# Some 230 pieces of a fused two-layer kernel at other places in the orders of five engines

## The reference

```python
h = layernorm(x)*(1+ca)+sa;  x = x + ga * attention(h)     # layer 0: 4 heads, dilations 1, 2, 4, 8
h = layernorm(x)*(1+cb)+sb;  x = x + gb * ffn(h)           # input and weight rounded to a 6-bit grid
h = layernorm(x)*(1+ca)+sa;  x = x + ga * mamba(h)         # layer 1
h = layernorm(x)*(1+cb)+sb;  x = x + gb * gated_recurrence(h)
# mamba: projection, convolution over 4 tokens, silu, then per channel (512) and state (16)
#   state = exp(dt*A)*state + dt*B*xc ;  y = sum over states of C*state
#   y = (y + D*xc) * silu(z) ; output projection
# gated_recurrence: over the 4 sequences b as steps:
#   c = sigmoid(wf x + uf c + bf)*c + sigmoid(wi x + ui c + bi)*tanh(wc x + uc c + bc)
#   out[b] = tanh(wo x[b] + uo c_final + bo)
```

## Time and profile before

| | |
|---|---|
| median of 3 runs | 1270.32 us (1268.75 to 1272.96) |
| span of the profiled execution | 1264.5 us, 12574 instructions |
| time of that execution beside its span | not recorded; median less span is 5.8 us |
| PE, DVE, POOL, ACT busy | 1140.8, 1155.2, 982.6, 795.0 us |
| mean granted clock of PE | 0.986 of full speed |
| first scan starts | 97.6 us |

### The profile page before, as it was taken

One profiled execution on the slowest core, in us unless ns is written; L12 is line 12 of the kernel. 1 busy time (PEld: TensorE's weight loads), 2 busy tenths in 40 slices (PEclk: granted clock), 3 DMA queues, 4 the chain that ended last, 5 costly groups with the idle time before them and its releaser, 6 DMA issues.

```text
span 1264.5 us, 12574 instructions
## 1 busy us (share of the span) xinstructions
PE 1140.8 (90%) x3612; PEld 640.1 (51%) x3612; DVE 1155.2 (91%) x1138; ACT 795.0 (63%) x1445; POOL 982.6 (78%) x712
## 2 busy tenths in 40 slices
PE   7989678998999899997999899997999899789996
PEld 5636333664457444764457443763457443444453
DVE  3768999999999999899999999899999999999987
ACT  2256567765786668755786668755786667655532
POOL 3216886889778887989778997889778996976862
PEclk9999989999999999999999999999999999899998
DMA  7308588766868688866878679876868786899922
GB/s 285 115 16 315 176 269 284 278 233 233 281 226 297 200 278 292 289 233 225 290 219 301 197 277 311 276 241 217 292 217 287 215 282 236 290 335 346 374 86 116
DMA packets 92309, 313.87 MB, mean 248 GB/s; under 512 B 10432, under 2 KB 15680, under 8 KB 91984
## 3 DMA queue, kind: packets, MB, share of 16 engines
q1 hardware_dynamic: 89936, 306.26, 70.3%
q10 hardware_dynamic: 2304, 6.82, 1.5%
HBM read 301.73 MB, written 11.31 MB: 248 GB/s over the span
## 4 chain that ended last, share of the span: by engine, by line
PE 43%; DVE 22%; POOL 14%; ACT 9%; issue 8%; DMA 3%; SPq 0%; DVEq 0%; POOLq 0%; ACTq 0%
PE ps L907 13%; DVE ps L1741 12%; POOL arena L1970 8%; PE ps L601 5%; PE ps L830 4%; PE ps L609 3%; DVE arena L1749 3%; DMA arena<-bc_scratch 2%; PE ps L647 2%; PE ps L751 2%; PE ps L723 2%; ACT ps L1295 2%; ACT arena L931 2%; PE ps L728 1%; PE ps L633 1%
## 5 line engine op out<-in xcount | busy, mean ns | idle before, releaser
L1970 POOL TENSOR_TENSOR arena<-arena 128x1024 f32<-128x1024 f32 x255 | 600.3, 2362 | 136.5 <-PE ps L907 113.2
L1741 DVE TENSOR_TENSOR_SCAN ps<-ps,arena 128x1024 f32<-128x1024 f32 (+1 forms) x257 | 585.8, 2280 | 30.3 <-ACT ps L1295 17.9
L907 PE MATMUL ps<-arena,identF 128*128 128x512 f32 x1024 | 482.8, 603 | 49.0 <-DVE arena L1749 29.4
L1295 ACT ACTIVATE ps<-arena,negA 128x512 f32<-128x512 f32 x512 | 332.7, 683 | 83.2 <-DVE arena L1749 78.2
L907 PEld LDWEIGHTS ps<-arena,identF 128*128 128x128 f32 x1024 | 190.3, 193 | 267.2 <-issue 208.8
L1749 DVE TENSOR_TENSOR arena<-ps,arena 128x1024 f32<-128x1024 f32 (+1 forms) x257 | 312.0, 1214 | 5.9
L922 ACT ACTIVATE arena<-arena,rnln 128x256 f32<-128x256 f32 x118 | 61.9, 589 | 42.1 <-POOL rnln L1776 24.9
L647 PE MATMUL ps<-arena,inw 128*128 128x512 f32 x128 | 60.0, 614 | 11.7 <-ACT arena L931 9.6
L1307 ACT ACTIVATE arena<-ps 128x2 f32<-128x2 f32 x128 | 22.0, 172 | 64.9 <-DVE arena L1749 64.4
L931 ACT ACTIVATE arena<-ps,modT 128x512 f32<-128x512 f32 x43 | 51.7, 1266 | 14.7 <-PE ps L474 12.6
L728 PE MATMUL ps<-arena,inw 128*128 128x512 f32 x128 | 60.2, 592 | 0.0
(11 more groups left out here) (222 smaller groups left out, 1707.1 us busy)
## 6 DMA issues: line engine op xcount, KB each, us to landing
arena<-bc_scratch SPq DMA_DIRECT2D x511, 512.0 KB, 5.0
arena<-in_x SPq DMA_DIRECT2D x16, 256.0 KB, 6.9
arena<-in_x SPq DMA_DIRECT2D x8, 512.0 KB, 8.4
xr_scratch<-arena SPq DMA_DIRECT2D x6, 512.0 KB, 6.9
px_scratch<-arena SPq DMA_DIRECT2D x6, 512.0 KB, 6.1
out_x<-arena SPq DMA_DIRECT2D x5, 512.0 KB, 2.6
arena<-bc_scratch SPq DMA_DIRECT2D x9, 256.0 KB, 3.6
woT<-in_woT SPq DMA_DIRECT2D x4, 512.0 KB, 10.0
```

The source lines that it names most:

```text
L907: x = pe.matmul(ps[:, Y, :], identF[:], inp[:, m % RING, q, :], start=False, stop=(i == BLOCK_STEPS - 1 and q == 1), skip_group_check=True)
L1295: x = act.activation(ps[:, 2 * (m % 2) + q, :], dt[:, kd, :], ACT.Exp, scale=negA[:, kd, 2 * i + q:2 * i + q + 1])
L1741: x = dve.tensor_tensor_scan(states, states, inp[:, m % RING, q, :].rearrange("p q t -> p (q t)"), 0.0, ALU.mult, ALU.add)
L1970: x = pool.tensor_tensor(inp[:, m % RING, :, :], u[:, kd:kd + 1, :].broadcast_to([P, 2, TH]), b_at[:, m % 3, :, :], ALU.mult)
```

## The change

Only the table `TIMES` is changed. It issues the same instructions; the pieces of the chains stand at other places in each engine's order. The part of the diff that the text speaks of:

```diff
 TIMES = {
-    "sp_before": {"x_in": -7, "bc_out": 30.5, "dt_in": 30.5},
-    "sp_after": {"xr_out": 11.75, "px_out": 28.25},
+    "sp_before": {"x_in": -7.25, "bc_out": 30, "dt_in": 21.75},
+    "sp_after": {"xr_out": 16.25, "px_out": 35.75},
...
-    "pe_before": {"hn1_t0": -2.25, "hn1_t1": -2.25, "q0": -2, "k0": -2, "s0": 2, "q1": 2, "k1": 3.75, "v0": 5.25,
-        "s1": 6, "att0": 7, "v1": 7, "att1": 10.25, "op0": 11, "op1": 11, "xd_t0": 20, "xd_t1": 20,
-    "pe_second": {"hn1_t0": 2.25, "hn1_t1": 2.25, "q0": 3, "k0": 3, "s0": 3, "q1": 3, "k1": 7.25, "v0": 8.25,
+    "pe_before": {"hn1_t0": -2.5, "hn1_t1": -15, "q0": -1.75, "k0": -4.75, "s0": 2.75, "q1": -10.5, "k1": 4.25,
+        "v0": 5.25, "s1": 6, "att0": 8, "v1": -10.25, "att1": 11.25, "op0": 11.5, "op1": -14, "xd_t0": 20, "xd_t1": 11,
+    "pe_second": {"hn1_t0": 3.25, "hn1_t1": 5, "q0": 1, "k0": 5.25, "s0": 1, "q1": -20.5, "k1": -2.5, "v0": 3,
+        "s1": -14.25, "att0": 7.75, "v1": 8, "att1": 10.25, "op0": 11, "op1": -1.5, "xd_t0": 19.5, "xd_t1": 4.25,
...
-    "act_before": {"hn1": (-3.5, -3.5), "hB1": (-2.25, -2.25), "q0": 0, "k0": 0, "q1": 3.25, "exp0a": 4.25,
-        "exp0b": 4.25, "k1": 4.25, "v0": 7, "exp1a": 7, "exp1b": 7, "att0": 9, "v1": 9, "att1": 10.75,
-        "x_proj": 28.75, "first_decay": (35, 37.75), "softplus": (33.75, 34.25), "dt_copy": 37.75, "xc_silu": 28.5},
-    "act_second": {"hn1": (-10.5, -10.5), "hB1": (6, 6), "q0": 6.25, "k0": 6.25, "q1": 7, "exp0a": 7,
-        "softplus": (33.75, 33.75), "dt_copy": 41.25, "xc_silu": 28.5},
+    "act_before": {"hn1": (-3.5, -11), "hB1": (-2.25, -19), "q0": -0.75, "k0": -3.75, "q1": 3.75, "exp0a": 1,
+        "exp0b": 1.25, "k1": -0.75, "v0": 6.5, "exp1a": 4.5, "exp1b": -8.25, "att0": 9.25, "v1": -7.25, "att1": 11.5,
+        "hn3": (24, 18.5), "hB3": (24.75, 16.25), "xc_init": (25.75, 23.75, 27.75, 24.5), "x_proj": 29.25,
+        "first_decay": (35.75, 42.25), "softplus": (34, 20.25), "dt_copy": 40.25, "xc_silu": 22.5},
+    "act_second": {"hn1": (-8.5, -19.25), "hB1": (6.5, 0.75), "q0": -2.5, "k0": 2, "q1": 5.25, "exp0a": -17,
+        "first_decay": (34.75, 51.25), "softplus": (34.25, 32.5), "dt_copy": 28, "xc_silu": 24.75},
...
-    "dve_before": {"ln1_stats": -4.5, "ln1_moments": -4, "smax": (2.5, 6.5), "rsum": (6.5, 8.75), "ln2_stats": 13.25,
-        "ln3_moments": 22.5, "pad": 25.75, "conv": (26.75, 26.75, 26.75, 28, 28, 28)},
-    "dve_second": {"ln1_stats": -13.5, "ln1_moments": -11.25, "smax": (6.75, 9), "rsum": (9, 9.5),
-    "dve_after": {"ln4_stats": 6.25, "z": (6.5, 7.75, 8.25, 9.75), "ln4_moments": 6.5},
+    "dve_before": {"ln1_stats": -3.75, "ln1_moments": -16.75, "smax": (2.5, 5.75), "rsum": (7, 7.5), "ln2_stats": 13,
+        "ln3_moments": 22.75, "pad": 12.5, "conv": (26.75, 16, 9.75, 28.25, 25.5, 23.5)},
+    "dve_second": {"ln1_stats": -9.25, "ln1_moments": -16.75, "smax": (-6.75, -11.5), "rsum": (6.75, 8.75),
+    "dve_after": {"ln4_stats": 6.25, "z": (5.5, 8, 8.5, 9.25), "ln4_moments": 6},
...
-        "ffn_add": (20, 20), "ln3_rstd": 22, "u": (35, 37), "cut": (35, 37)},
-    "pool_after": {"cp_gate": -7.25, "cp_add": (5, 5), "ln4_rstd": 6.75, "f_c": 21, "i_g": 25.5, "c_new": 25.5},
+        "ffn_add": (19.75, 15.25), "ln3_rstd": 22, "u": (33.75, 40.75), "cut": (35.25, 44.5)},
+    "pool_after": {"cp_gate": -10.25, "cp_add": (4.75, -22.5), "ln4_rstd": 6.25, "f_c": 20.25, "i_g": 26,
+        "c_new": 17.5},
```

33 lines of the change are left out of this document (16 added, 17 removed), and 11 rows, old and new, of the table TIMES.

## The result

The changed kernel takes 1277.24 us (median of 6 runs, 1275.79 to 1283.82) against 1269.53 us for the one before on the same chip (6 runs, 1267.51 to 1272.96): a ratio of 1.0074, 95% interval 1.0047 to 1.0101. It is slower; I had said 1267.7. They are more than the 7.7 between the medians: the traced execution of the kernel before was one of its fastest. Of its 70 executions beside the experiments three had a span under 1265 us; the median span on each of the four chips was 1266.7 to 1267.5.

What follows compares the result with a forecast made beforehand. DVE was taken to set the pace, its idle time being what could be won. 5.6 - 7.0 - 1.2 = -2.6 on the span 1264.5, plus 5.8, gave 1267.7 us; 8-in-10 range 1259 to 1277.

Steps and rivals of the forecast that it cites:

- Term 1: Start, first overlapped attention (half 1): chained evictions delay scans 0 and 1; +5.6 us by scan 8, between +3 and +9.
- The rule that I set beside it: Start, PE: after idling it runs at half rate, so waits between chained projections could add up to 2.9 us.
- term 2: Five steady seams, halves 2 to 6: three edits bring scan 28 forward; -1.4 us a seam, -7.0 in all.
- no drain: Seam's Exp table load: a skill rule gives 1.28 plus a drain, 2.66 us; the rows showed only 1.28.
- the sign of term 2: What would show the seam gain: a steady half of 142 us instead of 143.3.
- the gain stands: Steady seam to scan 40: saturated PE passes its earlier q0 on, coming 1.6 us earlier at the second c_proj.
- rival 2: ACT's order between decays 31 and 38 takes the seam back, 0.4 us lost a seam; 1277 us, chance 23%.
- I cost them at nothing: Other moved pieces (SP's later stores, POOL's gating, cuts): readers come 10 us later, so 0 us.
- Term 3: Seam of half 1: exponentials and copy leave decays 30 and 37, easing scan 30's 2.00 us wait; -1.2 us.
- The 5.8 us: Difference between profiled span 1264.5 and median 1270.32, taken as time lying around a span and added to the forecast.
- My range: Whole kernel: 1259 to 1277 us, meant to hold the time 8 times in 10.
- the sign: Whole kernel: the outcome that the change makes it slower, chance 23%.

Runs made afterwards that it cites:

- experiment 1: Kernel before with the changed table for half 1 alone: 1283.48 us; with z's entries of the block beside it changed too: 1275.03 us, ratio 1.0055.
- experiment 7: Kernel before with silu ahead of decay 24 and the next half's statistics behind the convolution's second part: 1268.15 us, ratio 0.9985; each alone: 1267.17 and 1274.72 us.
- Experiment 6: Changed kernel with the copy of dt and two small exponentials back at their old ScalarE place in halves 3, 5 and 7: 1282.31 us, ratio 1.0094.
- experiment 5: Changed kernel with SyncE's store of xr back: 1275.71 us; with all SyncE pieces and GpSimd's three weight gating products back: 1276.68 us, ratio 1.0063.
- experiment 3: Kernel before with the changed tables for the last block's output pieces (steps 224 to 255) alone: 1271.20 us, ratio 1.0017.

## Why the prediction was wrong

**Which part was right.** Term 1: 5.9 us at scan 8 for 5.6, and experiment 1 shows that the debt stays. That nothing gives it back was wrong by 1.1 us at step 16: a wait of 0.76 in the trace before, just ahead of scan 12, took a part. The rule that I set beside it (half rate for the other projections too, up to 2.9 us) did not come to pass for q1 and k1: these took 2.9 and 3.0 us at a granted clock of 1.00 (2.4 GHz), where I had put 2.9. In term 2 the step at scan 28 was right (-1.7 said, -2.0 measured), with its three edits and its chain through the columns, q0, the read-out and i_g. So were the waits that I listed after it: 1.4 at scan 32 (1.22 in the even halves, 1.42 in the odd ones), none at the gating product, 1.2 for the additions (1.62). Even the total at scan 40 was right: -1.4 said, -1.2 to -1.4 in all five seams. The table load costs 1.28 and the decay starts right behind it here too, with no drain (load at 641.38, decay at 642.67). And two halves show the 142 us that I had named as the sign of term 2, 142.3 for 143.6; the two with the DMA waits are longer than before (144.7 and 143.8 for 142.8).

**Which step failed first: "the gain stands".** I worked the seam out as far as scan 40 and took what stood there as lasting. Right behind scan 40 z2's product waits 0.50 us for its tanh, and 0.6 of the 1.4 is gone at scan 41; 0.4 to 0.7 is left at step 44. This makes a term of -3.0 for -7.0. The wait of 0.5 for the scores I had at 0, and of z2 I counted 0.3 ahead of scan 40. Counted to step 16 instead, the odd halves keep 1.5 and the even ones 0.8, but the odd ones' surplus is the quantising piece's, which I had not worked out. The argument behind "stands", that PE is saturated from q0 to the second c_proj and hands on what it gets, is not where it failed: in experiment 7 the seams' 1.9 to 2.0 us are all there at steps 40 and 44. Experiment 6 shows that the copy of dt, with which I argued for rival 2's upper end, costs nothing. Rival 2 gave nearly the measured time (1277), but out of other parts, so that was luck: seams that cost 0.4 each, where they win 0.6, and nothing for the loads and the last block.

**The step that cost most: "I cost them at nothing."** In the trace it was 6.8 of the 12.6 us between my sum (-2.6) and the +10.0: 2.1 between the seams and 4.7 in the last block. I excused SyncE's later stores by their readers having 10 us, and did not ask whose transfers they would now stand beside: rows of the scan, which land 3.8 us later (2.5 of it gone with the old order of the loads, experiment 5). And I never worked out the last block. I treated it as one more seam without attention, while there the same moves have nothing to hide behind: no next half's attention fills PE, and DVE has 98% in the earlier trace rows. The transposes and the gate matmuls put eight read-outs 2.7 us later behind their scan, and scan 238 waits 1.8 us for the input behind them; about 1 us of the 4.7 is the clock fall at step 234 and not the order's.

**Term 3** came out at +1.4 for -1.2. (The kernel of experiment 3, whose order there is the old one, shows +0.8 over the same steps, so the first part of this is not safely the change's.) The wait of 2.00 at scan 30 fell to 0.77 as said, but the read-out product at step 24 began to wait 1.64 for PE and scan 32 0.56; I had looked at one wait and not at what the other moved pieces put around it. DVE in that seam of the changed kernel:

```profile
220.23 0.69 DVE L1728 TENSOR_TENSOR arena<-ps,arena 128x512 f32<-128x512 f32 x1 [1.64 <-PE ps L908]
...
239.86 2.30 DVE L1742 TENSOR_TENSOR_SCAN ps<-ps,arena 128x1024 f32<-128x1024 f32 x1 [0.77 <-ACT ps L1296]
...
247.43 2.30 DVE L1742 TENSOR_TENSOR_SCAN ps<-ps,arena 128x1024 f32<-128x1024 f32 x1 [0.56 <-ACT ps L1296]
```

**The 5.8 us** that I put around the span were not that. An execution's time is 1.3 us above its span as a rule, 2.8 at most, in the 70 executions of the kernel before beside the experiments; the other 4.5 were the distance of a fast traced execution from the median. So the changed kernel's trace (1274.5) and median (1277.24) are 2.7 apart, and my sum missed the medians' change by 10.3 us (-2.6 for +7.7), not by 12.6.

My range ended at 1277.0, and the median lies 0.2 above: the sign was given 23%.

## What to carry to other kernels

Where one engine is the bound, subtract the starts of its repeated instruction between two traces: the steps of that difference name the places, and the totals by line do not. A wait that is listed is worth only what the next one behind it leaves, so price pairs, and treat blocks that occur once (the start, the last block) by themselves: no repetition averages them and nothing behind them pays back. Ask of the trace that you start from whether it is a typical execution: this one was 2 to 3 us shorter than the median span, and a wait that it happens to lack looks like a loss in every other trace. Pieces of a written-out order do not add: of the 15 kernels here, each with a part of the change or all but a part, six were slower than the whole of it by the median, two of them far beyond the intervals.
